# A gated convolution block over 16 images: channel strips in every half unit, the last five beside the second next image

## The reference

```python
# x: (16, 112, 112, 256) float32
x = x + conv0(gn(x), kernel)     # conv0: depthwise 3x3, both operands replaced by their signs
x = x + block1(gn(x), ...)       # gn: 32 groups of 8 channels, mean and variance over the image

# block1:
avg, mx = mean(x, (1, 2)), max(x, (1, 2))
xc = x * sigmoid(fc(avg) + fc(mx))             # one gate for each image and channel
m  = mean(xc, -1)                              # over channels, for each pixel
y  = s6(m, ...)                                # a scan over all pixels of an image
s  = conv7x7([mean(xc, -1), max(xc, -1)])
x2 = xc * sigmoid(y) + xc * sigmoid(s)
out = relu(batch_norm(x2))
```

## Time and profile before

| | us |
|---|---|
| median of 3 runs | 3651.7 (3645.94 to 3656.71) |
| span of the profiled execution | 3646.9 |
| its first stage, up to the last `max_rows` | about 1961 |

### The profile page before, as it was taken

The page is one execution under the profiler, slowest core; times in us unless marked ns, Lnnn a source line. Parts: engine busy times, 40 slices in busy tenths (PEclk is TensorE's granted clock), DMA queues, the critical chain, the costliest instruction groups (busy, mean ns, idle before and its releaser), DMA issues. The chain is left out here.

```text
span 3646.9 us, 51234 instructions
## 1 busy us (share of the span) xinstructions
PE 2669.1 (73%) x17009; PEld 1675.6 (46%) x17009; DVE 3209.0 (88%) x4441; ACT 2837.5 (78%) x4091; POOL 15.8 (0%) x17
## 2 busy tenths in 40 slices
PE   4889888988889888988876964333357676776766
PEld 3555555555555555555533311000045555555555
DVE  5899998998999989998995379999989999989897
ACT  3798788987898789877874248877778888888887
POOL 1000000000000000000000000000000000000000
PEclk8999999999999999999998655555577777777777
DMA  5898788988898889978773469999969999999998
GB/s 196 329 363 318 310 319 329 365 315 315 312 390 302 319 309 352 353 306 313 281 276 85 117 203 387 415 416 415 378 247 425 427 427 425 417 421 416 422 420 336
DMA packets 257267, 1228.01 MB, mean 337 GB/s; under 512 B 35757, under 2 KB 44425, under 8 KB 242729
## 3 DMA queue, kind: packets, MB, share of 16 engines
q1 hardware_dynamic: 257064, 1225.40, 85.7%
HBM read 805.14 MB, written 420.17 MB: 336 GB/s over the span
## 5 line engine op out<-in xcount | busy, mean ns | idle before, releaser
L921 PE MATMUL psum<-signs,taps 128*128 128x448 bf16 x4032 | 873.6, 365 | 106.1 <-DVE signs L646 68.5
L1532 PE MATMUL psum<-ident,xt 128*128 128x128 f32 x3136 | 558.3, 347 | 281.5 <-ACT stage L1566 229.7
L1532 PEld LDWEIGHTS psum<-ident,xt 128*128 128x128 f32 x3136 | 497.0, 211 | 368.5 <-ACT stage L1566 308.2
L921 PEld LDWEIGHTS psum<-signs,taps 128*128 128x128 bf16 x4032 | 392.8, 100 | 461.9 <-issue 109.7
L1074 PE MATMUL psum<-signs,picked 12*128 12x448 bf16 x896 | 329.5, 511 | 331.4 <-DMA signs<-gate_scratch 237.9
L1566 ACT ACTIVATE stage<-psum 128x512 f32<-128x512 f32 x784 | 406.2, 613 | 173.4 <-DMA out_dram<-stage 151.2
L1587 DVE SCALAR_TENSOR_TENSOR xc<-xt,curs,psum 128x1792 f32<-128x1792 f32 x224 | 456.2, 2078 | 84.7 <-PE psum L1074 81.9
L833 PE MATMUL psum<-ident,stage 128*128 128x128 f32 x3136 | 417.5, 276 | 102.6 <-ACT xt L448 63.0
L1358 DVE SCALAR_TENSOR_TENSOR xc<-xt,curs,psum 128x1792 f32<-128x1792 f32 x224 | 455.2, 2078 | 36.1 <-PE psum L1074 34.8
L1252 ACT ACTIVATE xc<-xc 128x1792 f32<-128x1792 f32 x224 | 380.0, 1697 | 98.3 <-DVE xc L1358 98.3
L494 ACT ACTIVATE xc<-xc,gbias,cur 128x896 f32<-128x896 f32 x420 | 448.4, 1123 | 0.0
(11 more groups left out here) (167 smaller groups left out, 2316.3 us busy)
## 6 DMA issues: line engine op xcount, KB each, us to landing
xt<-x_scratch SPq DMA_DIRECT2D x210, 1792.0 KB
stage<-x_dram SPq DMA_DIRECT2D x224, 896.0 KB, 9.3
out_dram<-stage SPq DMA_DIRECT2D x112, 1792.0 KB, 13.6
xc<-x_scratch SPq DMA_DIRECT2D x210, 896.0 KB, 8.3
x_scratch<-xt SPq DMA_DIRECT2D x208, 896.0 KB, 6.8
x_scratch<-last_unit SPq DMA_DIRECT2D x16, 896.0 KB, 8.5
xc<-ssm_scratch SPq DMA_DIRECT2D x28, 448.0 KB, 4.5
signs<-gate_scratch SPq DMA_DIRECT2D x217, 10.5 KB
```

Of the source, the lines that this page charges most:

```text
L921: ins = nc.tensor.matmul(turn[h % 2][:, b * 512:b * 512 + HB], taps[:, j, t, :], moving, start=t == 0, stop=t == 8)
L1532: last = nc.tensor.transpose(out_ps[k % 4][:, v * C + j * P:v * C + (j + 1) * P], block_in, ident[:, :])
```

## The change

- SP, ScalarE, VectorE and TensorE find the strip that belongs to a half unit with `strip_at(i, h, lag)`: it counts half units through all images, so strips follow each other without a break, one in each half unit, with lag 1 for the load, 3 for the gate, 4 for the maximum of the halves, 5 for sums, average and reductions. Strips 0 to 8 of image i-1 keep their half units in image i. The averages of strips 9 to 13 are now at h = 0 to 4 of image i+1.
- `channels_late` leaves the tail and the first half units. The tail holds no strip.
- `load_g` is called once in each half unit, after the store, with all its waits in it. Before, the first four strips were loaded together at the start of an image.
- The ring of four buffers runs on through the images (`ring`, `ring_turns`); the sums go to `turn[c % 2]` for all strips.
- `cur` and `gbias` are double, since two images' gates are in use at a time.
- `max_rows` moves from h = 3 to h = 5, and its result is stored at h = 7 and not at h = 4. In `blocks_back` the wait for it stands ahead of the second group of transposes alone.
- After image 15, strips 9 to 13 of image 14 are interleaved with the gate of image 15 and its first strips; the order of average and gate there shifts by one.

```diff
 hid = sb("hid", [NRED, 1])
-cur = sb("cur", [P, 2, NJ])
-gbias = sb("gbias", [P, NJ])
+cur2 = sb("cur", [P, 2, 2, NJ])
+cur = [cur2[:, b, :, :] for b in range(2)]
+gbias = sb("gbias", [P, 2, NJ])
 par = sb("par", [P, NB, 2 * NJ])
...
-    return (tile_ps if c >= 11 else turn[0 if c >= 9 else c % 2])[:, 0:SQ]
+    return turn[c % 2][:, 0:SQ]
+def strip_at(i, h, lag):
+    s = (i - 1) * NP + h - lag
+    return divmod(s, NP) if s >= 0 else None
+def ring(i, c):
+    return (i * NP + c) % 4
+def ring_turns(i, c):
+    return (i * NP + c) // 4 + 1
...
         def load_g(i, c):
-            sp.dma_start(xg[c % 4], x1_d[i, :, :, c * TP:(c + 1) * TP].rearrange("j c n -> c j n")
-                         ).then_inc(g_in[c % 4], 16)
-        def load_next_g(i, c):
-            sp.wait_ge(maxed, i * NP + c - 3)
-            sp.wait_ge(summed, i * NP + c - 3)
-            load_g(i, c)
+            for j in range(NJ):
+                sp.wait_ge(stored[c % NU][j], (i + 1) * 16)
+            if i == 0 and c == 0:
+                sp.wait_ge(bands_out, 16)
+            if i * NP + c >= 4:
+                sp.wait_ge(maxed, i * NP + c - 3)
+                sp.wait_ge(summed, i * NP + c - 3)
+            sp.dma_start(xg[ring(i, c)], x1_d[i, :, :, c * TP:(c + 1) * TP].rearrange("j c n -> c j n")
+                         ).then_inc(g_in[ring(i, c)], 16)
...
         def image(i):
-            more, channels = i + 1 < NB, i >= 1
+            more = i + 1 < NB
             if more:
...
                     load_x(i + 1, p)
-            if i >= 2:
-                sums_out(i - 2, NS - 2)
-                sums_out(i - 2, NS - 1)
-            if channels:
-                for u in range(NU):
-                    for j in range(NJ):
-                        sp.wait_ge(stored[u][j], i * 16)
-                if i == 1:
-                    sp.wait_ge(bands_out, 16)
-                if i >= 2:
-                    sp.wait_ge(maxed, (i - 1) * NP)
-                    sp.wait_ge(summed, (i - 1) * NP)
-                for c in range(4):
-                    load_g(i - 1, c)
             for h in range(NP):
...
                     store(i, (h - 1) // 2, (h - 1) % 2)
-                if h >= 5 and channels:
-                    load_next_g(i - 1, h - 1)
-                if h == 4 and i >= 2:
+                if at := strip_at(i, h, 1):
+                    load_g(*at)
+                if h % 2 == 0 and (at := strip_at(i, h, 6)):
+                    sums_out(at[0], at[1] // 2)
+                if h == 7 and i >= 2:
                     max_out(i - 2)
-                if h >= 6 and h % 2 == 0 and channels:
-                    sums_out(i - 1, (h - 6) // 2)
             store(i, NU - 1, NJ - 1)
-            if channels:
-                load_next_g(i - 1, NP - 1)
-                sums_out(i - 1, 4)
...
             image(i)
-        sums_out(NB - 2, NS - 2)
-        sums_out(NB - 2, NS - 1)
+        load_g(NB - 2, NP - 1)
+        for s in range(4, NS):
+            sums_out(NB - 2, s)
         max_out(NB - 2)
...
-            b = c % 4
+            b = ring(i, c)
             if c == 0:
                 act.wait_ge(gate_in, i + 1)
-            if resident and c >= 4:
+            if resident:
                 act.wait_ge(maxed, i * NP + c - 3)
                 act.wait_ge(summed, i * NP + c - 3)
-            if not resident:
-                act.wait_ge(g_in[b], i * (16 * turns(b, 4, NP)) + 16 * (c // 4 + 1))
+            else:
+                act.wait_ge(g_in[b], 16 * ring_turns(i, c))
             for j in range(NJ):
                 src = xt[:, j, c * TP:(c + 1) * TP] if resident else xg[b][:, j, :]
-                ins = nc.scalar.activation(xg[b][:, j, :], src, ACT.Identity, bias=gbias[:, j:j + 1],
-                                           scale=cur[:, 1, j:j + 1])
+                ins = nc.scalar.activation(xg[b][:, j, :], src, ACT.Identity, bias=gbias[:, i % 2, j:j + 1],
+                                           scale=cur[i % 2][:, 1, j:j + 1])
             ins.then_inc(gated, 1)
...
                 pack(i, h, first)
-                if h >= 5 and channels:
-                    average(i - 1, h - 5)
+                if h == 5 and i >= 2:
+                    max_rows(i - 2)
+                if at := strip_at(i, h, 5):
+                    average(*at)
                 if h >= 2 and more:
                     evacuate(i + 1, 2 * (h - 2) + 1)
-                if h == 0 and i >= 2:
-                    average(i - 2, 11)
-                    average(i - 2, 12)
-                if h == 1 and i >= 2:
-                    average(i - 2, 13)
-                if h == 3 and i >= 2:
-                    max_rows(i - 2)
                 if h == 0 and channels:
...
                     gate_exp(i - 1)
-                if h >= 3 and channels:
-                    apply_gate(i - 1, h - 3)
+                if at := strip_at(i, h, 3):
+                    apply_gate(*at)
...
             evacuate_next(1)
-            if channels:
-                average(i - 1, 9)
             evacuate_next(2)
             evacuate_next(3)
-            if channels:
-                average(i - 1, 10)
             square(i, NU - 1, 0, first)
             square(i, NU - 1, 1, first)
-            if channels:
-                apply_gate(i - 1, 11)
-                apply_gate(i - 1, 12)
-                apply_gate(i - 1, 13)
             inverse_deviation(i)
...
             image(i)
+        hidden(NB - 1)
+        apply_gate(NB - 2, 11)
+        average(NB - 2, 9)
+        gate_exp(NB - 1)
+        apply_gate(NB - 2, 12)
+        average(NB - 2, 10)
+        apply_gate(NB - 2, 13)
         average(NB - 2, 11)
+        apply_gate(NB - 1, 0, True)
         average(NB - 2, 12)
+        apply_gate(NB - 1, 1, True)
         average(NB - 2, 13)
         max_rows(NB - 2)
-        hidden(NB - 1)
-        gate_exp(NB - 1)
-        for c in range(NP):
+        for c in range(2, NP):
             apply_gate(NB - 1, c, True)
-            if c >= 1:
-                average(NB - 1, c - 1)
+            average(NB - 1, c - 2)
+        average(NB - 1, NP - 2)
         average(NB - 1, NP - 1)
...
             steps(nc.vector.tensor_copy(xmean, mean0[:, i % 2, :]))
-            if i >= 1:
-                reduce_blocks(i - 1, 10)
             dve.wait_ge(squared, i * (NS * NJ) + NS * NJ)
...
             steps(nc.vector.reciprocal(st[:, 14, :], st[:, 13, :]))
-            steps(nc.vector.tensor_tensor(cur[:, 1, :], rs, st[:, 14, :], ALU.mult))
-            steps(nc.vector.tensor_scalar(cur[:, 0, :], m1, -1.0, None, ALU.mult))
+            now = cur[i % 2]
+            steps(nc.vector.tensor_tensor(now[:, 1, :], rs, st[:, 14, :], ALU.mult))
+            steps(nc.vector.tensor_scalar(now[:, 0, :], m1, -1.0, None, ALU.mult))
             steps(nc.vector.tensor_copy(par[:, bass.ds((i + 1) % NB, 1), :],
-                                        cur[:, :, :].rearrange("p (o a) j -> p o (a j)", o=1)))
-            steps(nc.vector.tensor_tensor(gbias[:, :], cur[:, 0, :], cur[:, 1, :], ALU.mult))
+                                        now.rearrange("p (o a) j -> p o (a j)", o=1)))
+            steps(nc.vector.tensor_tensor(gbias[:, i % 2, :], now[:, 0, :], now[:, 1, :], ALU.mult))
             dve.sem_inc(gate_in, 1)
...
                 dve.wait_ge(max_turned, i * NRED_STEPS + 2 * (c - 1))
-            nc.vector.tensor_tensor(xm[c % 2], xg[c % 4][:, 0, :], xg[c % 4][:, 1, :], ALU.max
+            b = ring(i, c)
+            nc.vector.tensor_tensor(xm[c % 2], xg[b][:, 0, :], xg[b][:, 1, :], ALU.max
                                     ).then_inc(maxed, 1)
...
                     make_signs(i, u + 2, j)
-                if h >= 4 and channels:
-                    max_halves(i - 1, h - 4)
-                if h >= 5 and channels:
-                    reduce_blocks(i - 1, h - 5)
-                if h == 1 and i >= 2:
-                    reduce_blocks(i - 2, 13)
+                if at := strip_at(i, h, 4):
+                    max_halves(*at)
+                if at := strip_at(i, h, 5):
+                    reduce_blocks(*at)
                 add_convolution(i, u, j)
...
                     image_gate(i - 1)
-            if channels:
-                max_halves(i - 1, 10)
-                reduce_blocks(i - 1, 9)
             if more:
...
             image_variance(i)
-            if channels:
-                max_halves(i - 1, 11)
-                max_halves(i - 1, 12)
             attention_inputs(i)
-            if channels:
-                reduce_blocks(i - 1, 11)
-                reduce_blocks(i - 1, 12)
-                max_halves(i - 1, 13)
...
             image(i)
-        reduce_blocks(NB - 2, 13)
+        max_halves(NB - 2, 10)
+        reduce_blocks(NB - 2, 9)
         gate_argument(NB - 1)
         image_gate(NB - 1)
+        for c in range(11, NP):
+            max_halves(NB - 2, c)
+            reduce_blocks(NB - 2, c - 1)
         max_halves(NB - 1, 0)
```

(53 more changed lines are left out.)

## The result

The kernel after takes 3673.06 us (median of 5 runs), the kernel before, on the same chip, 3651.7 us. The ratio is 1.0058, with a 95% interval from 1.0044 to 1.0072: slower by 0.6%, 21 us, where 3653 us was forecast. The time lies inside the range of 3628 to 3675 us and on the side that had a chance of 0.28. In the kernel after it ends 19.8 us later than before, near the 21 us between the medians.

What follows compares the result with a forecast made beforehand. A relay bounds each image: VectorE's gate argument, then ScalarE and TensorE together, then VectorE alone. 8.75 + 79.15 + 15.8 + 14.45 = 118.15 us against 117.78; with first and last images +0.2, rounded up to 3653 us, range 3628 to 3675.

Steps and rivals of the forecast that it cites:

- Step 1, S to A': From S (sums of the next x) to A' (next image's last attention step): falls from 17.16 to 14.45 us.
- Step 2, A to the third convolution: From A (last attention step of the image ahead) to the third convolution: A + 8.75 us, earlier by 1.5.
- Step 3, the cost of full intervals: Third to last convolution: all eleven intervals become full ones, 77.7 us; the whole stretch 79.15 us, 5.3 longer.
- Step 3, `max_rows`: Its move to h=5: TensorE stalls 0.8 us, transposes wait another 0.3, the copy is 0.3; 1.45 in sum.
- the paragraph on SP's queue: Strip loads leave after each store and land within 14.4 us; other new waits met before; waits on stores taken at 0.
- Step 4, the tail: Last convolution to S: only four tiles turn through two banks, 15.8 us, saves 0.45.
- Image 15: Last image, turns no tiles and VectorE leads it: from 104.77 to 103.3 us, -1.5.
- image 1: Has no late strips of an earlier image, gains only in tail and statistics: -3.15 us.
- The drain: After image 15's attention, three more strips are gated: counted 0, between -2 and +4 us.
- The strips find room: Faster rival, chance 0.27: spread loads relieve the full DMA, the rhythm shrinks from 7.07 to 6.89 us; 26 less, 3627.
- The clock and the row of stalls: Slower rival, chance 0.28: TensorE's idle time in the tail or at h=5 lowers its clock; +20 us, 3673.
- It doesn't do what it says: Within the slower 0.28: convolutions 1 and 2 wait for averages 9 and 10, each image 1.5 us longer, 3672.

Runs made afterwards that it cites:

- e12_fill_only: The kernel after plus 54 unread transposes of the identity in each image's tail, filling TensorE's idle time: 3665.74 us, 1.0049 of the kernel before.
- e1_ring: The kernel after with the two row buffers of the averages (`srow`) alternating over the whole run: 3668.8 us, 1.0034 of the kernel before.
- e3_both: The kernel after with alternating row buffers and `max_rows` moved behind strip 0's sums, transposes and average: 3665.42 us, 1.0037 of the kernel before.
- e6_x_first_fill: `e3_both` plus SP issuing the next x tile ahead of the strip load, and 54 unread transposes in the tail: 3646.55 us, 0.9975 of the kernel before.
- e10_no_rows_move: `e6_x_first_fill` with `max_rows` back in the place that the change gave it: 3651.23 us, 0.9995 of the kernel before.
- e5_x_first: `e3_both` with SP issuing the next x tile right behind the store, ahead of the strip load: 3655.1 us, 1.0007 of the kernel before.
- e4_fill: `e3_both` with 54 unread transposes of the identity in TensorE's idle time in the tail: 3652.03 us, 1.0008 of the kernel before.
- e9_before_care: The kernel before with the x load ahead of the strip load and 20 unread transposes behind the variance's sum: 3642.41 us, 0.9979 of the kernel before.
- e8_before_x_first: The kernel before with only SP's order changed, the x load ahead of the strip load: 3650.49 us, 1.0001 of the kernel before.

## Why the prediction came out as it did

- **Step 1, S to A'** (14.45): right, 14.51. The reductions and the two maxima of the earlier trace rows are gone from the chain.
- **Step 2, A to the third convolution** (8.75): right, 8.64. It is 8.12 where the clock stays up (`e12_fill_only`), so half a microsecond of it is the clock of the first convolution. A part of the lower clock was in the term, taken from the earlier trace rows.
- **Step 3, the cost of full intervals** (7.06 each, 21.2 for three): right to 0.2 us, 49.36 / 7 = 7.05 and 21.02. The new order buys no cheaper strip.
- **Step 3, `max_rows`** (1.45): this is the term that was too small; 9.81 - 7.06 = 2.75 us was measured. The stall of TensorE was foretold at 0.8 and is 1.23 us in that image, and the copy is there. (The term's own sums are loose: 7.6 + 8.7 + 2 x 7.31 is 30.9, not 31.1, and 0.8 + 0.3 + 0.3 is 1.4.) What the term lacks is ScalarE's wait for the transfer out of `srow`. The prediction dismissed it with "The other new waits of the queue are met before". It had looked at the waits that the diff adds to SP, not at an old wait of ScalarE whose distance the diff shortens: from four half units to one. The interval came out 1.3 us longer than forecast, 17 us over 13 images, and `e1_ring`, with 8.67 us, shows that this wait is what fills it.
- **The wait's removal does not give these 17 us.** `e1_ring` gained 4 us and `e3_both` 8. The chain over VectorE, SP and the last x tile ends S at the same A + 105. For that second chain the paragraph on SP's queue had no term; it followed strip loads and not the x loads behind them. In the prediction's own sum, without the first wait, S would have been at A + 103.7; `e6_x_first_fill`, with the later place of `max_rows`, the earlier tile and the fill, reaches 103.2, and `e10_no_rows_move` 103.7.
- **Step 4, the tail** (15.8): 15.93 at full clock, 0.1 over; the mean is 16.31. In six of 13 images it is 16.06 to 17.29, where transposes of the last two tiles run in part at 1.2 GHz after an idle time of 2.99 us. Timeline of TensorE, kernel after: 14 transposes in 2.82 us, where the 14 ahead took 1.72.

```profile
1090.13 1.72 PE L820 MATMUL psum<-ident,stage 128*128 128x128 f32 x14 [1.27 <-ACT xt L448]
...
1094.84 2.82 PE L820 MATMUL psum<-ident,stage 128*128 128x128 f32 x14 [2.99 <-ACT xt L448]
```

- **The whole.** Image 15 gained 1.07 of the 1.5 us forecast, image 1 2.65 of 3.15. The drain costs 0.5 us: from the last attention to the last reductions 1979.82 - 1934.80 = 45.02 against 44.55, near the 0 that was taken.
- **The rivals.** "The strips find room" is wrong at its root: DMA share 1.01 in the middle, and the rhythm is unchanged. "The clock and the row of stalls" named the right side and nearly the time (3673), by another mechanism. Its own mechanism is there, but in some images only, and a fill of the idle time in the kernel after (`e12_fill_only`) gives back 7 us, not 20. So it is partly luck that the time lies in the range: its upper end was set for this rival, and the wait on `srow` stood in none of the cases. "It doesn't do what it says" did not occur; step 2 gained what it should.

What stays open: why the same idle time of 2.99 us lowers the clock in some images and not in others (tails above 16 us in 6 of 13 in the kernel after, in 11 of 13 in `e5_x_first`), and how the landing time of the last x tile, 7.1 to 14.6 us over the runs, depends on what else is under way. No run separates these.

**The net balance.** Between the third and the last convolution the new order costs 5.6 us (80.19 against 74.61), at the start and in the statistics of an image it saves 4.1, and the tail is 0.3 longer. It gives VectorE 5.7 us of idle time in one piece, and nothing in this order uses it. With the repairs the new order is at 3646.6 us (0.9975 of the kernel before) and the old one at 3642.4 (0.9979): they are alike within about 0.1%, and a gain of the order itself was not found.

## What to carry to other kernels

When a change moves work closer together, list every buffer that the moved steps write and count the half units between its two users before and after, waits that the diff doesn't touch included; a ring of two, numbered anew in each image and with an odd number of users in it, has its last and first user in the same buffer. When a stall is found, ask for the next chain of the same length before it is priced: here 19 us were expected of a wait's removal, and it gave 4. And give the old kernel the same repairs before a gain is put down to the new order.

## What the runs showed of the hardware

A small strided transfer took some 6 us while the DMA engines were full. The transfer out of `srow` (7.0 KB) is issued at 1025.64, and the wait for it ends 6.46 us later, with a DMA share of 1.01 over that stretch. No run has the same transfer with the engines free, so what the load adds to it is open. The Trainium skill (DMA: Bandwidth & Descriptors, "Anatomy of one DMA — SWDGE (gpsimd) path") gives a fixed cost of some 2.0 us for a transfer of another path; the trace of this one, issued by SP, shows about three times that up to the end of the wait. The Trainium skill (Perfetto Trace Analysis, "Optimization Strategy") says that the same gap in a repeating stretch can mean too few buffers. The trace has such a gap, 12 waits in 12 images, and none is left in `e1_ring`; but the number of buffers was right there, and only their numbering wrong.

TensorE's clock stays up longer with work whose result nobody reads. Granted clock and busy times of 300 to 1700 us, of the kernel before, after, and of `e12_fill_only`, which is the kernel after with the fill alone (columns as in the earlier trace rows):

```profile
300.00:1700.00 1400.00, 1202.25 (x9299) 760.33 (x9297) 1288.22 (x2455) 1175.71 (x1904) 0.00 (x0) 0.95 0.86 330
```

```profile
300.00:1700.00 1400.00, 1191.45 (x9188) 755.26 (x9186) 1265.84 (x2409) 1162.05 (x1886) 0.00 (x0) 0.94 0.87 327
```

```profile
300.00:1700.00 1400.00, 1252.52 (x9832) 826.57 (x9831) 1272.53 (x2425) 1164.73 (x1887) 0.00 (x0) 0.98 0.88 328
```

54 transposes of the identity in each image raise the mean from 0.94 to 0.98 here, from 0.93 to 0.97 in `e4_fill` (against `e3_both`) and from 0.93 to 0.99 in `e6_x_first_fill` (against `e5_x_first`). They bought 13 us in `e4_fill`, 9 in `e6_x_first_fill`, and 7 in `e12_fill_only`, where a wait took part of it back; 20 transposes bought about 8 in `e9_before_care` (against `e8_before_x_first`). So a fill of idle time was worth 0.2 to 0.4% in a kernel whose TensorE is not its most loaded engine.
